# One tap column of a shifted sum: an identity matmul on TensorE against an add on VectorE at PSUM eviction

## The chip, the cores and the metric

The kernel runs on one core of a Trainium2 chip. The metric is the device time of one execution in microseconds (us). The kernel before was timed three times: 4166.49, 4167.12 and 4171.71 us, median 4167.12 us. A fourth execution was profiled.

## What is computed

The input x has shape (4, 128, 128, 128): 4 images, 128 channels, 128 rows of 128 pixels, float32. Two "metaformer" layers follow. Only the first convolution matters here, cut from the reference:

```python
offset = conv3x3(ln_c(x), w_off)            # 18 channels: 9 taps x (dy, dx)
py, px = base_y + dy, base_x + dx           # per tap and pixel
sampled = bilinear_gather(ln_c(x), py, px)  # (B, C, 9, H, W)
x = x + einsum("bckhw,ock->bohw", sampled, w_conv)
# then: a routed mixture of experts, a Fourier mixing, a second expert stage
```

The offsets are a 3x3 convolution with 18 outputs. For one output pixel it is a sum over three tap rows ky and three tap columns kx. The term of tap column kx must be moved by kx-1 pixels along the row.

## The kernel before

The program has phases that run one after the other: a setup, phase A (normalisation, offsets, sampling and the first convolution; up to about 2146 us of the span), a test for far offsets, phase BC and phase DE. The change lies in phase A alone.

**Phase A** works on NG = 128 groups G of four image rows, 32 groups for each image. Pixels of a row lie on the 128 partitions. The function order_a (L169) writes one list of stages with slots of time, and each engine's function (tensor, scalar, vector, gpsimd, sync) walks through that one list and issues its own stages in that order. So each engine's instructions stand in a fixed order, and semaphores join the engines. A step s of the list lasts 12 slots, 18 where the chunk of sampled rows has six rows rather than four (at the end of an image), and touches several groups at once:

- turn, stats, scale, norm and conv for group F = s+4. TensorE transposes the rows into PSUM (L312, tile TK), VectorE takes their statistics (L458, L461), ScalarE writes the normalised rows (L379). TensorE multiplies the rows with the offset weights (L321: 162 = 9 taps x 18 columns) into YB[0] and YB[1]. ScalarE takes them out, scaled, into the ring yr (L406).
- zsum, shift, offs, offs_out, reach, place and hats for group Z = s+2. GpSimd adds the three tap rows of yr into zz (L534, L540), which keeps three tap columns of 18 values for each of 4 rows. TensorE multiplies each tap column with a shift matrix and adds the three in PSUM, tile OF (L330, 72 columns = 4 rows x 18). ScalarE copies OF to on (L417) and sends it to memory (L392). VectorE reduces on to a maximum and a minimum (L467, L468), GpSimd places it into the ring oc (L568, L576) and forms the interpolation weights hh (L552, L555). ScalarE takes their absolute value (bend, L422), VectorE clips them (L473).
- prod and turn_s for the chunk of group N = s+1: VectorE (even rows, L481) and GpSimd (odd rows, L521) multiply the weights into sx, VectorE transposes each into tt (L490).
- sample: TensorE multiplies windows of the normalised image with tt into SB (L351), three parts a quad of rows. ScalarE copies SB to the ring sr (L443).
- out, residual and x1_out for group s-2: nine matmuls of 512 columns into OB (L366), then VectorE adds the input (L496).

The shift matrices come from constants(): shift[:, kx, :] has ones where row x+kx-1 meets column x. For kx = 1 that is the unit matrix.

YO is one PSUM bank that holds YB[1] in columns 0 to 323 and OF in columns 324 to 395 (L261 to L263). So shift waits until ScalarE has emptied YB (y_ready), and conv with h = 1 waits until OF has been taken out (on_ready). The stages around the change before:

```python
elif o[0] == "shift":                      # TensorE, L324
    w.wait_ge(z_step, z_count[G]); w.wait_ge(on_ready, G)
    w.wait_ge(y_ready, 4 * min(G + 2, NG))
    for kx in range(3): matmul(OF, shift[:, kx, :], zz[:, G % 2, :, kx, :])
elif o[0] == "offs":                       # ScalarE, L411
    w.wait_ge(shifted, G + 1); w.wait_ge(on_out[G % 2], 16 * (G // 2))
    w.wait_ge(oc_ready, G - 1); w.wait_ge(reached, 2 * (G - 1))
    copy(on[:, G % 2], OF).then_inc(on_ready, 1)
```

zz and on have two buffers each. GpSimd's zsum of group G waits for shifted of group G-2, since it overwrites that group's zz.

Of the kernel before, what the change touches and what calls it, by code (L numbers as in the profile page):

```python
# [10 lines left out]
ALU = mybir.AluOpType  # L11
# [231 lines left out]
def phase_a(nc, ctx, ins, k, xtp, offd, x1d):  # L243
# [6 lines left out]
    zz = S("a_zz", [128, 2, 4, 3, 18])  # L250
    on = S("a_on", [128, 2, 4, 18])
# [17 lines left out]
    def sem(name):  # L269
        sems.append(ctx.enter_context(nc.semaphore("a_" + name)))  # L270
        return sems[-1]
# [2 lines left out]
    turned, convolved, shifted, sampled, conv_out = (  # L274
        sem(n) for n in ("turned", "convolved", "shifted", "sampled", "conv_out"))

    normed, y_ready, on_ready, bent, sr_ready = (sem(n) for n in ("normed", "y_ready", "on_ready", "bent", "sr_ready"))

    filled, bn_done, mv_ready, reached, clipped, weighed_dve, turned_s, x1_ready = (
        sem(n) for n in ("filled", "bn_done", "mv_ready", "reached", "clipped", "weighed_dve", "turned_s", "x1_ready"))  # L280

    rs_step, z_step, oc_ready, hats_ready, weighed_pool = (
        sem(n) for n in ("rs_step", "z_step", "oc_ready", "hats_ready", "weighed_pool"))
# [3 lines left out]
    on_out = [sem(f"on_out{i}") for i in range(2)]  # L287
# [15 lines left out]
    def tensor(e):  # L303
        w = Once(e)
        for o in order:
            if o[0] == "turn":
                G = o[1]
                w.wait_ge(x_in[G % NX], 16 * (G // NX + 1))
                w.wait_ge(mv_ready, G)
                w.wait_ge(normed, 2 * G)  # L310
                for r in range(4):
                    t = e.transpose(TK[:, r, :], xin[:, G % NX, r * 128:(r + 1) * 128], k["ident"][:, :])  # L312
                t.then_inc(turned, 1)
            elif o[0] == "conv":
                _, G, h = o
                w.wait_ge(y_ready, 4 * (G - 1) + 2 * h + 2)
                if h:

                    w.wait_ge(on_ready, min(G - 2, NG - 1) + 1)
                for r in range(2):  # L320
                    t = e.matmul(YB[h][:, r, :], xin[:, G % NX, (2 * h + r) * 128:(2 * h + r + 1) * 128],  # L321
                                 k["wof"][:, :], start=True, stop=True)
                t.then_inc(convolved, 1)
            elif o[0] == "shift":  # L324
                G = o[1]
                w.wait_ge(z_step, z_count[G])
                w.wait_ge(on_ready, G)
                w.wait_ge(y_ready, 4 * min(G + 2, NG))
                for kx in range(3):
                    t = e.matmul(OF[:, :, :], k["shift"][:, kx, :], zz[:, G % 2, :, kx, :], start=(kx == 0),  # L330
                                 stop=(kx == 2))
                t.then_inc(shifted, 1)
            elif o[0] == "sample":


                _, Q, h = o
                m_ = quad(Q)[1]
                for j in range(2):
                    w.wait_ge(win_in[half_of(Q, j) % NWH], win_count[half_of(Q, j)])
                w.wait_ge(filled, 1)  # L340
                w.wait_ge(turned_s, quad(Q)[0] + m_)
                w.wait_ge(sr_ready, 3 * Q + h)
                for i in range(NWIN // 3):
                    for j in range(2):
                        for q in range(4):
                            u = NU_ * (NWIN // 3 * h + i)
                            m = tt[32 * q:32 * q + 32, Q % NTP, 1152 * j + u:1152 * j + u + 1]

                            m = bass.AP(m.tensor, m.offset, [list(m.ap[0]), [96, 3 * m_], [31, 3], [1, NU_]])
                            d = SB[:, q, 0:432].rearrange("p (k t x) -> p k t x", k=12, t=3)  # L350
                            t = e.matmul(d[:, 0:3 * m_, :, NU_ * i:NU_ * i + NU_],  # L351
                                         win[32 * q:32 * q + 32, half_of(Q, j) % NWH, NWIN // 3 * h + i, :], m,
                                         start=(j == 0), stop=(j == 1))
                t.then_inc(sampled, 1)
            elif o[0] == "out":
                _, G, t_ = o
                w.wait_ge(x1_ready, G)
                w.wait_ge(sr_ready, 3 * quad_of(last_centre(G)) + 3)
                kr, kx = divmod(t_, 3)
                a = (4 * G - 2) % NSR  # L360
                ob = OB[:, :].rearrange("p (r x) -> p r x", r=4)

                m = 4 if a + 4 <= NSR else 2 + kr
                for y, r, m in [(a, 0, m)] + ([(a + m - NSR, m, 4 - m)] if m < 4 else []):
                    rows = sr[:, y * 1152:(y + m) * 1152].rearrange("p (r t x) -> p r t x", r=m, t=9)
                    t = e.matmul(ob[:, r:r + m, :], k["wcv"][:, 3 * (2 - kr) + kx, :], rows[:, :, t_, :],  # L366
                                 start=(t_ == 0 and r == 0), stop=(t_ == 8))
                if t_ == 8:
                    t.then_inc(conv_out, 1)

    def scalar(e):
        w = Once(e)
        for o in order:
# [20 lines left out]
            elif o[0] == "y_out":  # L394
                _, G, h = o
                b, q = divmod(G, GI)
                for r in (2 * h, 2 * h + 1):
                    y = 4 * q + r
                    k0, k1 = max(0, 1 - y), min(3, H + 1 - y)
                    w.wait_ge(convolved, 2 * G + r // 2 + 1)  # L400
                    if G >= 3:
                        w.wait_ge(z_step, z_count[G - 3 if r < 3 else G - 2])
                    for first, slot, m in runs(b * H + y - 1 + k0, k1 - k0, NYR):
                        kr = first - (b * H + y - 1)
                        d = slot * 162 + kr * 54
                        a = e.activation(yr[:, d:d + 216 * m].rearrange("p (k f) -> p k f", f=216)[:, :, 0:54],  # L406
                                         YB[r // 2][:, r % 2, 54 * kr:54 * (kr + m)].rearrange(
                                             "p (k f) -> p k f", f=54),
                                         ACT.Identity, bias=k["zero"][:, 0:1], scale=rs[:, G % 2, 4 + r:5 + r])
                    a.then_inc(y_ready, 1)  # L410
            elif o[0] == "offs":  # L411
                G = o[1]
                w.wait_ge(shifted, G + 1)
                w.wait_ge(on_out[G % 2], 16 * (G // 2))
                w.wait_ge(oc_ready, G - 1)
                w.wait_ge(reached, 2 * (G - 1))
                e.copy(on[:, G % 2, :, :], OF[:, :, :]).then_inc(on_ready, 1)  # L417
            elif o[0] == "bend":
                G = o[1]
                v = hh[:, G % 2, 0:len(chunk(G))].rearrange("p c t i -> p (c t i)")  # L420
                w.wait_ge(hats_ready, G + 1)
                e.activation(v, v, ACT.Abs).then_inc(bent, 1)  # L422
            elif o[0] == "sample":
                _, Q, h = o
                n, m_ = quad(Q)
                b, c = centre(n)
                R = b * H + c - 1
                w.wait_ge(sampled, 3 * Q + h + 1)
                w.wait_ge(conv_out, (min(R + m_ + 1, b * H + H - 1) - NSR) // 4 + 1)

                if c < 0:
                    parts = [(0, 1, 2, 1), (1, 1, 1, 2), (2, 2, 0, 3)]
                elif m_ < 4:
                    parts = [(0, 1, 0, 2), (1, 1, 0, 1)]
                else:
                    parts = [(0, 4, 0, 3)]
                for kx in range(3):
                    x = max(0, 12 * h - kx)
                    m = min(31, 12 * h + 11 - kx) + 1 - x
                    for i, ni, kr, nk in parts:  # L440
                        d = sr[:, ((R - 2) % NSR + i + kr) * 1152 + kr * 384 + kx * 128 + x:][:, 0:1]
                        v = SB[:, 0, (9 * i + 3 * kr + kx) * 12 + x + kx - 12 * h:][:, 0:1]
                        a = e.copy(bass.AP(d.tensor, d.offset, [list(d.ap[0]), [1152, ni], [1536, nk], [32, 4], [1, m]]),  # L443
                                   bass.AP(v.tensor, v.offset, [list(v.ap[0]), [108, ni], [36, nk], [512, 4], [1, m]]))
                a.then_inc(sr_ready, 1)

    def vector(e):
# [4 lines left out]
        for o in order:  # L452
            if o[0] == "stats":
# [5 lines left out]
                for i in range(4):  # L459
                    w.wait_ge(bn_done, 4 * G + i + 1)  # L460
                    a = e.bn_aggr(mv[:, G % 2, i, :], st[:, G % 2, i, :])  # L461
                a.then_inc(mv_ready, 1)
            elif o[0] == "reach":
                G = o[1]
                w.wait_ge(on_ready, G + 1)
# [32 lines left out]
    def gpsimd(e):  # L498
        w = Once(e)
        for o in order:  # L500
# [24 lines left out]
            elif o[0] == "zsum":  # L525
# [3 lines left out]
                z = zz[:, G % 2, :, :, :].rearrange("p r k f -> p r (k f)")  # L529
                n = z_count[G]  # L530
                w.wait_ge(y_ready, 4 * G + (5 if q < GI - 1 else 4))
                w.wait_ge(shifted, G - 1)
                if q < GI - 1:
                    e.tensor_tensor(z, v[:, :, 0, :], v[:, :, 1, :], ALU.add).then_inc(z_step, 1)  # L534
                else:
# [1213 lines left out]
```

## Time and profile before

| | before |
|---|---|
| median of 3 runs | 4167.12 us (4166.49 to 4171.71) |
| profiled execution, its own time | 4168.03 us |
| its span | 4166.2 us |
| mean granted TensorE clock | 0.957 of full speed |
| TensorE matmul busy | 3877.1 us (93%) |
| VectorE busy | 2583.8 us (62%) |
| ScalarE busy | 1772.6 us (43%) |
| GpSimd busy | 1585.4 us (38%) |

The times are of whole executions; the span is from the first to the last instruction of the profiled one. Busy time is the time in which an engine had an instruction under way. TensorE's granted clock has two levels here, 1.0 (2.4 GHz) and 0.5 (1.2 GHz). A float32 matmul stands in the trace as two matmul records and two weight loads, so the three matmuls of a shift are six of each.

### The profile page before, as it was taken

The numbers are of one execution on the slowest core, as the hardware profiler recorded it, in microseconds if no ns is written. First come the engines' busy times: TensorE is split into PE (matmuls) and PEld (weight loads), VectorE is DVE, ScalarE is ACT, GpSimd is POOL, SyncE is SP. The second block draws the span as 40 slices with busy tenths as digits, with TensorE's granted clock in tenths as the row PEclk, the third lists the DMA queues.
The fourth block names the chain that finished last, engine by engine and source line by source line (L and its number), as shares of the span: only waits on it lengthen the run. The fifth ranks groups of instructions, "written<-read, shape, count | busy, mean of one in ns | idle before, by whom it ended". The sixth has DMA issues, their size and how long they took to land. (4 is left out here: it accounts for less than half of the span.)

```text
span 4166.2 us, 90514 instructions
## 1 busy us (share of the span) xinstructions
PE 3877.1 (93%) x32471; PEld 2569.3 (62%) x32471; DVE 2583.8 (62%) x8765; ACT 1772.6 (43%) x4557; POOL 1585.4 (38%) x2857
## 2 busy tenths in 40 slices
PE   4999999999999999999978999999999999986458
PEld 4666666666666666666644555666666666654245
DVE  3444434444444444444428888999999999986634
ACT  3555545555555555555511111333333333356124
POOL 3544445454454544544412222332323232344210
PEclk8999999999999999999989999999999999999755
DMA  5544454444554544545416666777777777754869
GB/s 126 93 89 92 88 88 91 90 90 90 92 92 89 91 90 92 92 87 94 76 56 244 244 246 257 258 261 264 257 268 254 268 257 267 252 174 124 335 263 395
DMA packets 602226, 705.73 MB, mean 169 GB/s; under 512 B 61088, under 2 KB 484768, under 8 KB 585392
## 3 DMA queue, kind: packets, MB, share of 16 engines
q1 hardware_dynamic: 496304, 625.97, 52.6%
q10 hardware_dynamic: 104448, 71.85, 5.7%
q8 instruction: 258, 4.23, 0.5%
q14 instruction: 192, 1.57, 0.1%
q0 software_dynamic: 1024, 2.10, 0.1%
HBM read 519.10 MB, written 179.54 MB: 168 GB/s over the span
## 5 line engine op out<-in xcount | busy, mean ns | idle before, releaser
L366 PE MATMUL a_ob<-a_sr,wcv 128*128 128x512 f32 (+3 forms) x2820 | 1084.4, 519 | 0.8 <-DVE a_xo L496 0.8
L443 ACT COPY a_sr<-a_sb 128x576 f32<-128x576 f32 (+7 forms) x1296 | 620.9, 562 | 914.8 <-PE a_sb L351 906.6
L351 PEld LDWEIGHTS a_sb<-a_tt,a_win 32*128 32x128 f32 x19008 | 655.6, 185 | 260.0 <-issue 244.6
L351 PE MATMUL a_sb<-a_tt,a_win 32*128 32x144 f32 x19008 | 748.2, 300 | 14.5 <-ACT a_sr L443 13.1
L521 POOL TENSOR_TENSOR a_sx<-a_hh 128x576 f32<-128x576 f32 x260 | 378.5, 1456 | 927.3 <-DVE a_hh L473 919.2
L366 PEld LDWEIGHTS a_ob<-a_sr,wcv 128*128 128x128 f32 x2820 | 493.2, 192 | 279.6 <-issue 231.2
L473 DVE TENSOR_SCALAR a_hh<-a_hh 128x576 f32<-128x576 f32 (+1 forms) x128 | 59.5, 465 | 944.0 <-ACT a_hh L422 944.0
L1075 DVE TENSOR_TENSOR b_P<-b_P,b_x 128x1024 f32<-128x1024 f32 x512 | 620.0, 1212 | 0.1
L985 PE MATMUL b_z<-b_P,b_ew 128*128 128x512 f32 x1024 | 475.0, 607 | 0.0
L1206 POOL TENSOR_TENSOR b_ss<-b_st 128x12 f32<-128x12 f32 (+2 forms) x167 | 35.2, 211 | 1124.5 <-DVE b_pp L1150 993.5
L988 PE MATMUL b_z<-b_P,b_ew 128*128 128x512 f32 x1024 | 460.3, 592 | 0.0
L490 DVE STREAM_TRANSPOSE a_tt<-a_sx 128x576 f32<-128x576 f32 x520 | 401.8, 773 | 21.2 <-POOL a_sx L521 12.2
L988 PEld LDWEIGHTS b_z<-b_P,b_ew 128*128 128x128 f32 x1024 | 194.6, 190 | 206.1 <-issue 201.4
L1222 POOL TENSOR_TENSOR b_rs<-b_ss,mhalf 128x12 f32<-128x12 f32 (+2 forms) x167 | 312.4, 1871 | 13.2 <-POOL b_ss L1218 0.2
L1048 ACT ACTIVATE c_tn<-c_x,b_rs 128x128 f32<-128x128 f32 x512 | 163.6, 390 | 349.2 <-POOL b_rs L1222 348.2
L985 PEld LDWEIGHTS b_z<-b_P,b_ew 128*128 128x128 f32 x1024 | 184.5, 190 | 200.1 <-issue 184.8
L379 ACT ACTIVATE a_tn<-a_tk,a_rs 128x128 f32<-128x128 f32 x512 | 195.7, 485 | 8.8 <-POOL a_rs L513 8.8
L481 DVE TENSOR_TENSOR a_sx<-a_hh 128x576 f32<-128x576 f32 x260 | 193.9, 746 | 4.3
L1419 PE MATMUL d_b<-ident,e_x 128*128 128x128 f32 x512 | 137.5, 425 | 47.3 <-DMA e_x<-x3d 46.4
L496 DVE TENSOR_TENSOR a_xo<-a_ob,a_xin 128x512 f32<-128x512 f32 x128 | 88.4, 690 | 122.0 <-PE a_ob L366 122.0
L967 PE MATMUL b_rd<-b_iw,b_x 128*128 128x136 f32 x1024 | 153.8, 294 | 5.5 <-DVE b_lr L1100 3.5
L982 PE MATMUL b_z<-b_pT,b_ebm 32*128 32x128 f32 x1024 | 148.5, 284 | 0.0
(181 smaller groups left out, 5406.3 us busy)
## 6 DMA issues: line engine op xcount, KB each, us to landing
b_P<-pd SPq DMA_DIRECT2D x128, 2048.0 KB, 7.4
a_win<-xtp SPq DMA_DIRECT2D x2144, 36.0 KB
a_xin<-in_x SPq DMA_DIRECT2D x128, 256.0 KB, 5.9
xtp<-a_tn ACTq DMA_DIRECT2D x128, 256.0 KB, 2.3
x1d<-a_xo SPq DMA_DIRECT2D x128, 256.0 KB, 5.7
b_x<-x1d SPq DMA_DIRECT2D x128, 256.0 KB, 7.7
x2d<-b_xa SPq DMA_DIRECT2D x128, 256.0 KB, 2.8
d_wb<-in_w SPq DMA_DIRECT2D x16, 2048.0 KB, 18.8
```

Source lines behind the costliest of these rows:

```text
L351: t = e.matmul(d[:, 0:3 * m_, :, NU_ * i:NU_ * i + NU_], win[32 * q:32 * q + 32, half_of(Q, j) % NWH, NWIN // 3 * h + i, :], m, start=(j = ...
L366: t = e.matmul(ob[:, r:r + m, :], k["wcv"][:, 3 * (2 - kr) + kx, :], rows[:, :, t_, :], start=(t_ == 0 and r == 0), stop=(t_ == 8))
L379: a = e.activation(tn[:, G % NTN, r, :], TK[:, r, :], ACT.Identity, bias=rs[:, G % 2, r:r + 1], scale=rs[:, G % 2, 4 + r:5 + r])
L443: a = e.copy(bass.AP(d.tensor, d.offset, [list(d.ap[0]), [1152, ni], [1536, nk], [32, 4], [1, m]]), bass.AP(v.tensor, v.offset, [list(v.ap ...
L481: e.tensor_tensor(sx[:, n % NST, :, 0:NI * NJ].rearrange("p t (j i) -> p t j i", j=NJ), hh[:, G % 2, i, :, None, 0:NI].to_broadcast([128, ...
L490: e.transpose(tt[:, Q % NTP, 0:2304].rearrange("p (j a t x) -> p a t j x", j=2, a=4, t=9)[:, n - quad(Q)[0]], sx[:, n % NST, :, :].rearran ...
L521: e.tensor_tensor(sx[:, n % NST, :, 0:NI * NJ].rearrange("p t (j i) -> p t j i", j=NJ), hh[:, G % 2, i, :, None, 0:NI].to_broadcast([128, ...
L985: e.matmul(ZE[u][:, :, :], ew[:, x, :], P[:, G % NPB, :, x, :], start=False, stop=False)
L988: t = e.matmul(ZE[u][:, :, :], ew[:, x, :], P[:, G % NPB, :, x, :], start=False, stop=(x == 7))
L1048: f = e.activation(tn3[:, u, r, :], x3t[:, G % 3, r, :], ACT.Copy, scale=rs[:, (G + LAG) % 2, 8 + r:9 + r])
L1075: t = e.tensor_tensor(v, v, x1[:, G % NX1, r, None, :].to_broadcast([128, 8, 128]), ALU.mult)
L1222: e.tensor_tensor(rs[:, u, c], ss[:, u, 2, c], k["mhalf"][:, c], ALU.pow).then_inc(scaled, 1)
```

## The change

TensorE multiplies only tap columns 0 and 2 with their shift matrices. The stage offs moves from ScalarE to VectorE, where it becomes one tensor_tensor: OF plus zz[:, G % 2, :, 1, :], written to on. The waits of offs stay the same; on_ready is now VectorE's. GpSimd's zsum waits for on_ready of group G-2 instead of shifted. Nothing else moves.

```diff
             elif o[0] == "shift":
                 G = o[1]
                 w.wait_ge(z_step, z_count[G])
                 w.wait_ge(on_ready, G)
                 w.wait_ge(y_ready, 4 * min(G + 2, NG))
-                for kx in range(3):
+                for kx in (0, 2):
                     t = e.matmul(OF[:, :, :], k["shift"][:, kx, :], zz[:, G % 2, :, kx, :], start=(kx == 0),
                                  stop=(kx == 2))
                 t.then_inc(shifted, 1)
...
     def scalar(e):
-            elif o[0] == "offs":
-                G = o[1]
-                w.wait_ge(shifted, G + 1)
-                w.wait_ge(on_out[G % 2], 16 * (G // 2))
-                w.wait_ge(oc_ready, G - 1)
-                w.wait_ge(reached, 2 * (G - 1))
-                e.copy(on[:, G % 2, :, :], OF[:, :, :]).then_inc(on_ready, 1)
...
     def vector(e):
+            elif o[0] == "offs":
+                G = o[1]
+                w.wait_ge(shifted, G + 1)
+                w.wait_ge(on_out[G % 2], 16 * (G // 2))
+                w.wait_ge(oc_ready, G - 1)
+                w.wait_ge(reached, 2 * (G - 1))
+                e.tensor_tensor(on[:, G % 2, :, :], OF[:, :, :], zz[:, G % 2, :, 1, :], ALU.add).then_inc(on_ready, 1)
...
     def gpsimd(e):   # zsum
                 w.wait_ge(y_ready, 4 * G + (5 if q < GI - 1 else 4))
-                w.wait_ge(shifted, G - 1)
+                w.wait_ge(on_ready, G - 1)
```

VectorE's own order in a regular step, before (a_xo is the residual, a_sx the product, a_tt the transposed product, fm the maxima and minima):

```order
L496 TENSOR_TENSOR a_xo<-a_ob,a_xin 128x512 [waits a_x1_out0,a_conv_out]
L490 STREAM_TRANSPOSE a_tt<-a_sx 128x9x2x32 [waits a_weighed_pool]
L481 TENSOR_TENSOR a_sx<-a_hh 128x576 [waits a_turned_s]
L490 STREAM_TRANSPOSE a_tt<-a_sx 128x9x2x32 [waits a_weighed_dve]
L467 TENSOR_REDUCE fm<-a_on 128x1 [waits a_on_ready]
L468 TENSOR_REDUCE fm<-a_on 128x1
L490 STREAM_TRANSPOSE a_tt<-a_sx 128x9x2x32 [waits a_weighed_pool]
```

And the same place of a regular step with the change:

```order
L498 TENSOR_TENSOR a_xo<-a_ob,a_xin 128x512 [waits a_x1_out0,a_conv_out]
L492 STREAM_TRANSPOSE a_tt<-a_sx 128x9x2x32 [waits a_weighed_pool]
L464 TENSOR_TENSOR a_on<-a_yo,a_zz 128x72 [waits a_oc_ready,a_reached,a_on_out1,a_shifted]
L483 TENSOR_TENSOR a_sx<-a_hh 128x576 [waits a_turned_s]
L492 STREAM_TRANSPOSE a_tt<-a_sx 128x9x2x32 [waits a_weighed_dve]
L469 TENSOR_REDUCE fm<-a_on 128x1 [waits a_on_ready]
L470 TENSOR_REDUCE fm<-a_on 128x1
```

The eviction now stands between the second transpose and the second product, and it carries the wait for TensorE's shift. ScalarE's order before, in the middle of a regular step:

```order
L443 COPY a_sr<-a_sb 128x4x3x4x10
L417 COPY a_on<-a_yo 128x72 [waits a_oc_ready,a_reached,a_on_out1,a_shifted]
L392 DMA offd<-a_on 128x72 [waits a_on_ready]
L443 COPY a_sr<-a_sb 128x4x3x4x12 [waits a_sampled]
L443 COPY a_sr<-a_sb 128x4x3x4x12 x2
```

And with the change:

```order
L438 COPY a_sr<-a_sb 128x4x3x4x10
L394 DMA offd<-a_on 128x72 [waits a_on_ready]
L438 COPY a_sr<-a_sb 128x4x3x4x12 [waits a_sampled]
L438 COPY a_sr<-a_sb 128x4x3x4x12 x2
```

The copy is gone from ScalarE; the DMA to memory stays in its place and waits for VectorE.

## Rows read from the trace of the kernel before

**Rows 1.** The page: busy time by engine, and granted clock in 40 slices.
```profile
PE 3877.1 (93%) x32471; PEld 2569.3 (62%) x32471; DVE 2583.8 (62%) x8765; ACT 1772.6 (43%) x4557; POOL 1585.4 (38%) x2857
...
PEclk8999999999999999999989999999999999999755
```

**Rows 2.** Stretches of phase A: busy time by engine, clock, DMA share, GB/s.
```profile
1000.00:1500.00 500.00, 497.75 (x5805) 340.44 (x5807) 216.32 (x558) 267.91 (x644) 240.03 (x359) 1.00 0.50 91
...
566.00:582.00 16.00, 13.75 (x209) 11.49 (x208) 5.58 (x16) 5.20 (x32) 4.43 (x9) 0.71 0.56 78
...
1090.00:1106.00 16.00, 13.76 (x241) 9.80 (x243) 6.43 (x17) 5.38 (x32) 6.28 (x11) 1.00 0.56 85
```

**Rows 3.** TensorE's timeline: start, us, instruction; one regular step and two image ends.
```profile
554.12 0.89 PE L330 MATMUL a_yo<-a_zz,shift 128*128 128x72 f32 x6
...
570.33 1.57 PE L351 MATMUL a_sb<-a_tt,a_win 32*128 32x72 f32 x48 [0.92 <-ACT a_sr L443]
...
599.01 0.89 PE L330 MATMUL a_yo<-a_zz,shift 128*128 128x72 f32 x6
...
1004.52 2.74 PE L366 MATMUL a_ob<-a_sr,wcv 128*128 128x512 f32 x6
1007.19 1.88 PE L351 MATMUL a_sb<-a_tt,a_win 32*128 32x144 f32 x48
...
1014.58 0.89 PE L330 MATMUL a_yo<-a_zz,shift 128*128 128x72 f32 x6
1015.30 2.80 PE L366 MATMUL a_ob<-a_sr,wcv 128*128 128x256 f32 x12
1018.04 1.89 PE L351 MATMUL a_sb<-a_tt,a_win 32*128 32x144 f32 x48
...
1025.01 0.82 PE L321 MATMUL a_yo<-wof,a_xin 128*128 128x162 f32 x4
...
1028.77 1.89 PE L351 MATMUL a_sb<-a_tt,a_win 32*128 32x144 f32 x48
1030.59 0.89 PE L330 MATMUL a_yo<-a_zz,shift 128*128 128x72 f32 x6
...
1078.54 0.89 PE L330 MATMUL a_yo<-a_zz,shift 128*128 128x72 f32 x6
...
1117.60 0.66 PE L330 MATMUL a_yo<-a_zz,shift 128*128 128x72 f32 x4
```

**Rows 4.** TensorE's weight loads in the same regular step.
```profile
1014.58 0.74 PEld L330 LDWEIGHTS a_yo<-a_zz,shift 128*128 128x128 f32 x6 [0.16 <-issue]
1015.24 2.46 PEld L366 LDWEIGHTS a_ob<-a_sr,wcv 128*128 128x128 f32 x12
```

**Rows 5.** All instructions of L330, and what TensorE waited for until 2200 us.
```profile
L330 PE MATMUL a_yo<-a_zz,shift x768: 272/275/489, 47.2 to 2082.9; 128*128 128x72 f32 x192
...
PE a_sb L351 <- ACT a_sr L443: 13.1, 15, 1.6
...
PE a_yo L330 <- POOL a_zz L540: 9.0, 5, 4.3
```

**Rows 6.** ScalarE's timeline in the regular step.
```profile
1014.72 1.62 ACT L443 COPY a_sr<-a_sb 128x576 f32<-128x576 f32 x3 [3.19 <-PE a_sb L351]
1016.20 0.26 ACT L417 COPY a_on<-a_yo 128x72 f32<-128x72 f32 x1
1016.49 0.36 ACTq L392 DMA_DIRECT2D offd<-a_on  x1
1020.00 1.76 ACT L443 COPY a_sr<-a_sb 128x576 f32<-128x576 f32 x3 [3.54 <-PE a_sb L351]
...
1024.59 0.69 ACT L422 ACTIVATE a_hh<-a_hh 128x576 f32<-128x576 f32 x1
```

**Rows 7.** VectorE's timeline in the regular step, then GpSimd's last weights.
```profile
1012.87 0.69 DVE L496 TENSOR_TENSOR a_xo<-a_ob,a_xin 128x512 f32<-128x512 f32 x1 [0.55 <-PE a_ob L366]
1013.48 0.77 DVE L490 STREAM_TRANSPOSE a_tt<-a_sx 128x576 f32<-128x576 f32 x1
1014.17 0.75 DVE L481 TENSOR_TENSOR a_sx<-a_hh 128x576 f32<-128x576 f32 x1
...
1016.49 0.23 DVE L467 TENSOR_REDUCE fm<-a_on 128x1 f32<-128x72 f32 x1 [0.75 <-ACT a_on L417]
...
1016.77 0.77 DVE L490 STREAM_TRANSPOSE a_tt<-a_sx 128x576 f32<-128x576 f32 x1
1025.30 0.46 DVE L473 TENSOR_SCALAR a_hh<-a_hh 128x576 f32<-128x576 f32 x1 [7.76 <-ACT a_hh L422]
...
1017.50 0.70 POOL L555 TENSOR_TENSOR a_hh<-a_oc,cy 128x288 f32<-128x288 f32 x1
```

**Rows 8.** The nearest VectorE add of PSUM and SBUF with few elements (setup, L61).
```profile
L61 DVE SCALAR_TENSOR_TENSOR wof<-s_t,wraw x1: 327/327/327, 3.6 to 3.6; 128x162 f32<-128x162 f32 x1
```

More of the change, by code:

```diff
@@ L275, in phase_a @@
         sem(n) for n in ("turned", "convolved", "shifted", "sampled", "conv_out"))
-    normed, y_ready, on_ready, bent, sr_ready = (sem(n) for n in ("normed", "y_ready", "on_ready", "bent", "sr_ready"))
-    filled, bn_done, mv_ready, reached, clipped, weighed_dve, turned_s, x1_ready = (
-        sem(n) for n in ("filled", "bn_done", "mv_ready", "reached", "clipped", "weighed_dve", "turned_s", "x1_ready"))
+    normed, y_ready, bent, sr_ready = (sem(n) for n in ("normed", "y_ready", "bent", "sr_ready"))
+    filled, bn_done, mv_ready, on_ready, reached, clipped, weighed_dve, turned_s, x1_ready = (
+        sem(n) for n in ("filled", "bn_done", "mv_ready", "on_ready", "reached", "clipped", "weighed_dve", "turned_s", "x1_ready"))
     rs_step, z_step, oc_ready, hats_ready, weighed_pool = (
```

## Prediction

> **What bounds the kernel now.** I read the page first. TensorE is busy 93% of the span, the other engines 62% or less [rows 1], but that is a mean over phases, and the change lies in phase A. So I cut phase A into stretches. From 1000 to 1500 us TensorE is busy 497.75 of 500 us at the full clock, while VectorE has 216, ScalarE 268 and GpSimd 240 us of work [rows 2]. The timeline shows how regular it is: the shift of one step starts at 1014.58 us and the next at 1030.59 us, 16.01 us a step, with matmuls back to back between [rows 3]. What TensorE waits for up to 2200 us is short: 13.1 us for ScalarE's copies of the samples, at the start and at the ends of images, and 9.0 us for GpSimd's sum in five early steps [rows 5]. So in phase A almost every nanosecond taken from TensorE's row of work is a nanosecond off the time, and work given to VectorE costs nothing as long as nobody on TensorE's side waits for it.
>
> **What the removed matmul is worth.** There are 768 matmul records of L330 [rows 5], six a step, so 128 steps and three matmuls of two records in each. One matmul in three goes: 256 records and 256 weight loads. The 275 ns that a record lasts [rows 5] is no price, since records overlap. The price is the spacing. Two views give it. The first weight load of the shift starts at 1014.58 and the first of the next group at 1015.24: 0.66 us for six loads, 0.11 us each [rows 4]. The first matmul record starts at 1014.58 and the next group's at 1015.30: 0.72 us for six, which includes the step into the group [rows 3]. Taking two records from the middle leaves the step into the group in place, so I take the loads' spacing: 0.66 / 3 = 0.22 us a step. By the other view it is 0.72 / 3 = 0.24 us. The lower bound is a price by columns alone: three 512-column matmuls (six records) take 1007.19 - 1004.52 = 2.67 us, 0.89 us each [rows 3], and 72 / 512 of that is 0.125 us.
>
> The page "TensorE: Matmul & The Clock Gate" of the Trainium skill has both rules side by side. In "Back-to-back issue gap" a warm matmul costs its columns over 2.4 GHz plus 2.5 ns, in "LDWEIGHTS" a load costs its weight columns over 1.2 GHz. With two passes a record, as the 512-column rows imply, the first rule makes a record 62.5 ns and the removal 16 us; the second makes a load 107 ns and the removal 27 us. The spacing of 0.11 us in this trace sides with the second.
>
> Not all 128 steps count. In the first four, before 90 us, TensorE waits for GpSimd's sum, and a shorter matmul only lengthens a wait somewhere. I take them at nothing. 124 x 0.22 = **27.3 us less**. With 0.24 us and all 128 steps it is 30.7 us, the upper bound; with 0.125 us and 128 steps 16.0 us, the lower.
>
> **What is added to VectorE.** One add a step of 72 elements, PSUM plus SBUF. The trace has none of this size. The nearest rows are L61 with 162 elements, 327 ns [rows 8], and the residual with 512 elements, 0.69 us [rows 7]. The line through both is (690 - 327) / 350 = 1.04 ns an element, which gives 327 - 90 x 1.04 = 0.23 us for 72. Nothing to 0.33 us are the bounds. The wait is the larger thing. VectorE's order is fixed, and the add stands between a transpose that ends near 1014.2 us and the product of L481 that started at 1014.17 us [rows 7]. The shift's last record ended at 1015.47 us [rows 3] and will end some 0.22 us earlier. So VectorE stands still for about 1.0 us, adds until about 1015.5 us, and product, transpose, maxima and last transpose slip by about 1.2 us. The last transpose, now 1016.77 to 1017.54 us, ends near 1018.8 us. Who waits for it on TensorE is the first sample part of the next quad, at 1028.77 us [rows 3]: 10 us to spare. VectorE's next work, the clipping, waits for ScalarE until 1025.30 us anyway, after 7.76 us of idleness [rows 7]. I cost this at nothing; its cover is that idle stretch. GpSimd's product for the odd row uses the same two sx buffers and waits for the transposes; it has the same 10 us.
>
> **What leaves ScalarE.** The copy of 0.26 us at 1016.20 us goes [rows 6]. It was followed by 3.54 us of waiting for TensorE's next sample, so it was hidden: nothing. on_ready comes at about 1015.5 us instead of 1016.46 us. Those behind it (the DMA of the offsets, GpSimd's placing and weights, which ended at 1018.20 us, the bend at 1024.59 us [rows 6, 7]) have their data earlier or at the same time. TensorE's own wait for on_ready stands at the second conv, 1025.01 us [rows 3], 9 us later. GpSimd's changed wait asks for a group two steps back, which has long been done.
>
> **At the ends of images** ScalarE's copies hold TensorE up for up to 0.92 us at a time [rows 3]. The stall is between a sample and its copy, whose distance does not change; the time gained earlier is carried through it. VectorE will stand there up to 7 us behind the shift, and the work behind the add has over 10 us to its sample.
>
> **The sum** against the profiled execution: 4168.03 - 27.3 = 4140.7 us. Its time is 0.9 us above the median of the three runs, 4167.12 us, which gives 4139.8. I say **4140 us**. A difference of 0.2%, 8.3 us, is about what a measurement of this kernel can tell from none.
>
> One term is chance. At the first image end the granted clock was down (mean 0.71), at the second it was not (1.00), with the same idle times of TensorE [rows 2]. From shift to shift over two steps that was 599.01 - 554.12 = 44.89 us against 1117.60 - 1078.54 = 39.06 us [rows 3]: 5.8 us for one drop. The change moves every later image end against whatever sets the clock, so one drop more or less is possible: plus or minus 5.8 us. The three runs lie 5.2 us apart, about one such drop.
>
> **The rivals.**
> 1. *The columns are the price.* If the loads could hide, the removed matmul is worth 0.125 us and the time is 4168.0 - 16.0 = 4152 us. For it: the 512-column rows follow their columns. Against: the loads of this very group are spaced evenly at 0.11 us, and the two remaining matmuls have the same form. Chance 5%.
> 2. *Another wait takes its place.* TensorE finishes its step sooner and then waits for a ScalarE copy, a window's DMA or the residual, and the step stays at 16.0 us: 4168 us. For it: such waits appear as soon as samples follow each other closely (0.92 us at an image end [rows 3]). Against: in a regular step the copies end at 1016.34 us and the next sample starts at 1018.04 us [rows 3, 6], 1.7 us to spare against 0.22; the residual ends at 1013.56 us, and its reader starts at 1015.30 us. Chance 3%.
> 3. *VectorE's new wait reaches TensorE.* Each step VectorE stands 1.0 us and works 0.23 us more. If product and transpose were the last thing that TensorE's next quad waits for, that would be exposed: 124 x 1.23 - 27.3 = 125 us, 4293 us, slower. It decides once those instructions run more than the 10 us late that now lie between last transpose and sample. A lock between VectorE and GpSimd would push that way; GpSimd's product lies beside VectorE's. The page "SBUF — State Buffer" of the Trainium skill, "Who interferes with whom", says that a VectorE instruction with two SBUF inputs and a GpSimd one that reads SBUF exclude each other, and that one with a single SBUF input, as the new add, does not; no row here shows the add. Against the rival: one more product's length is under 2 us, far from 10. Chance 2%.
>
> **How the numbers follow.** 90% for the forecast, 5, 3 and 2% for the rivals. Its own range goes from all 128 steps at 0.24 us with one clock drop less (4168.0 - 30.7 - 5.8 = 4131.5) to 27.3 us less with one drop more (4146.5). The rivals are within the 2 in 10 that may be left out, so the range is 4131.5 to 4147. Faster by over 0.2%: the forecast and rival 1, 95%. Within 0.2%: rival 2, 3%. Slower: 2%.
>
> **What would show it.** L332 with 512 records spaced as before; steps of 15.79 us, shift to shift, instead of 16.01; TensorE still busy for over 99% of a regular stretch; the add at about 0.23 us, with an idle time of about 1 us before it that ends with TensorE; ScalarE's copy gone and its waits for samples as long as before. It would be wrong if steps shorten by 0.13 us (rival 1), if TensorE's waits for ScalarE or DMA grow to some 27 us (rival 2), or if its first sample of a quad waits for VectorE's transposes (rival 3).

## The result and the profile after

| | before | changed |
|---|---|---|
| median of 4 runs each | 4169.41 us (4166.49 to 4172.17) | 4146.88 us (4145.19 to 4148.28) |
| ratio, 95% interval | | 0.9948 [0.9934, 0.9963] |
| profiled execution | 4168.03 us | 4145.51 us |
| its span | 4166.2 us | 4143.7 us |
| mean granted TensorE clock | 0.957 | 0.951 |

The change is faster by 22.5 us; the forecast was 27.3 us and a time of 4140 us. The measured median stands 7 us above that, at the very top of the range. Of these 7 us, 4.8 are a smaller gain. The rest is the base: the forecast started from 4167.12 us, and a fourth run of the kernel before moved its median to 4169.41 us. The regular steps of phase A did what was forecast. What was sized wrongly lies at the ends of the images.

The page of the changed kernel, busy time and clock (answers to [rows 1]):

```profile
PE 3865.7 (93%) x32215; PEld 2550.6 (62%) x32215; DVE 2631.6 (64%) x8893; ACT 1758.8 (42%) x4429; POOL 1597.5 (39%) x2857
...
PEclk8999999999999999999979999999999999999755
```

TensorE has 256 matmul records less, VectorE 128 instructions more and ScalarE 128 less. TensorE's timeline in two regular steps (start, us, instruction; answers to [rows 3]):

```profile
997.39 0.67 PE L332 MATMUL a_yo<-a_zz,shift 128*128 128x72 f32 x4
997.90 2.80 PE L368 MATMUL a_ob<-a_sr,wcv 128*128 128x256 f32 x12
...
1013.18 0.67 PE L332 MATMUL a_yo<-a_zz,shift 128*128 128x72 f32 x4
...
1028.93 0.67 PE L332 MATMUL a_yo<-a_zz,shift 128*128 128x72 f32 x4
```

From shift to shift it is 15.79 and 15.75 us, where it was 16.01 and 15.97 us: 0.22 us a step, the spacing of two weight loads. From the shift to the next group's first record it is 0.51 us now and was 0.72 us [rows 3]. The add on VectorE, all 128 of them, and what VectorE did around it in the regular step (answers to [rows 7]):

```profile
L464 DVE TENSOR_TENSOR a_on<-a_yo,a_zz x128: 193/233/235, 45.1 to 2058.2; 128x72 f32<-128x72 f32 x128
```
```profile
996.30 0.77 DVE L492 STREAM_TRANSPOSE a_tt<-a_sx 128x576 f32<-128x576 f32 x1
998.10 0.23 DVE L464 TENSOR_TENSOR a_on<-a_yo,a_zz 128x72 f32<-128x72 f32 x1 [1.03 <-PE a_yo L332]
998.25 0.93 DVE L483 TENSOR_TENSOR a_sx<-a_hh 128x576 f32<-128x576 f32 x1
999.21 0.78 DVE L492 STREAM_TRANSPOSE a_tt<-a_sx 128x576 f32<-128x576 f32 x1
...
1000.15 0.77 DVE L492 STREAM_TRANSPOSE a_tt<-a_sx 128x576 f32<-128x576 f32 x1
```

The wait of 1.03 us and the add of 0.23 us are the forecast numbers. The last transpose ends at 1000.9 us; TensorE's first sample of the next quad starts at 1011.37 us, still 10 us later. What TensorE waited for from 90 to 2100 us is one line:

```profile
PE a_sb L353 <- ACT a_sr L438: 6.6, 7, 1.0
```

So in this profile no wait took the removed matmul's place, on VectorE or anywhere.

**Where the time went.** I cut both spans at events that both have: the fifth and the last shift, the last residual, the first add of phase BC (L1075, now L1077) and the end. Differences are taken before rounding.

| stretch | before, us | changed, us | difference |
|---|---|---|---|
| start to fifth shift | 90.6 | 88.1 | -2.5 |
| fifth to last shift, 123 steps | 1991.8 | 1969.4 | -22.3 |
| last shift to start of last residual | 67.9 | 66.3 | -1.6 |
| last residual to first add of phase BC | 41.6 | 41.8 | +0.2 |
| first add of phase BC to the end | 1974.3 | 1978.1 | +3.8 |

In the second line 123 steps at 0.22 us should give 27.1 us. What is missing is at the image ends. The three inner ones, two steps each from shift to shift, took 44.89, 39.06 and 39.55 us before, and take 42.35, 42.32 and 42.44 us now: 3.6 us more instead of six times 0.22 us less, so 4.9 us in all. The reason stands in the clock column (ninth from the left: busy time of PE, PEld, DVE, ACT, POOL, then the granted clock). Three stretches of 150 us around the three ends, of before and then of the changed kernel:

```profile
500.00:650.00 150.00, 147.75 (x1715) 103.03 (x1710) 65.00 (x165) 76.07 (x205) 71.15 (x107) 0.95 0.50 89
1000.00:1150.00 150.00, 147.75 (x1797) 102.02 (x1795) 64.16 (x165) 78.91 (x212) 70.64 (x108) 1.00 0.51 91
1530.00:1680.00 150.00, 147.30 (x1795) 102.00 (x1794) 63.81 (x164) 78.10 (x208) 69.87 (x106) 1.00 0.50 92
```
```profile
500.00:650.00 150.00, 148.12 (x1761) 102.64 (x1763) 66.29 (x172) 77.52 (x201) 70.01 (x103) 0.97 0.51 91
1000.00:1150.00 150.00, 148.12 (x1770) 101.91 (x1768) 66.11 (x171) 77.38 (x201) 69.83 (x105) 0.97 0.51 90
1530.00:1680.00 150.00, 148.12 (x1746) 101.73 (x1748) 66.04 (x172) 77.41 (x201) 70.32 (x108) 0.97 0.50 91
```

Before, the clock fell to half at one end of three; now it falls at all three. The single drop of before was also the longer one: it took the mean of its stretch to 0.95, each drop of the changed kernel took it to 0.97.

The tail's 1.6 us go with the clock as well. TensorE from the last shift to the last residual, before, changed, and changed once more (e5 below):

```profile
2082.33:2150.26 67.93, 65.25 (x652) 41.68 (x648) 12.12 (x20) 17.63 (x47) 7.98 (x7) 0.92 0.14 30
2057.52:2123.82 66.30, 63.60 (x650) 40.33 (x646) 12.60 (x20) 17.51 (x46) 8.02 (x7) 0.95 0.14 31
2050.77:2115.75 64.98, 62.28 (x650) 39.07 (x646) 12.60 (x20) 17.50 (x46) 8.03 (x7) 0.97 0.14 31
```

The same work, but for the one matmul, took 67.9 us at a mean clock of 0.92, 66.3 us at 0.95 and 65.0 us at 0.97.

### The profile page after: what moved, and what is told of

It reads as the page before. It is cut to its first block and busy times, and to the rows that moved or that the text cites. A ratio compares the mean times of both kernels' runs of the same rounds, so it can differ in the third digit from the quotient of the medians.

```text
span 4143.7 us, 89876 instructions
## 1 busy us (share of the span) xinstructions
PE 3865.7 (93%) x32215; PEld 2550.6 (62%) x32215; DVE 2631.6 (64%) x8893; ACT 1758.8 (42%) x4429; POOL 1597.5 (39%) x2857
## 5 line engine op out<-in xcount | busy, mean ns | idle before, releaser
L1077 DVE TENSOR_TENSOR b_P<-b_P,b_x 128x1024 f32<-128x1024 f32 x512 | 620.2, 1212 | 0.1
L987 PE MATMUL b_z<-b_P,b_ew 128*128 128x512 f32 x1024 | 486.4, 619 | 0.0
L990 PE MATMUL b_z<-b_P,b_ew 128*128 128x512 f32 x1024 | 460.3, 592 | 0.0
L483 DVE TENSOR_TENSOR a_sx<-a_hh 128x576 f32<-128x576 f32 x260 | 225.2, 866 | 4.3
```

Source lines behind the costliest of these rows:

```text
L483: e.tensor_tensor(sx[:, n % NST, :, 0:NI * NJ].rearrange("p t (j i) -> p t j i", j=NJ), hh[:, G % 2, i, :, None, 0:NI].to_broadcast([128, ...
L987: e.matmul(ZE[u][:, :, :], ew[:, x, :], P[:, G % NPB, :, x, :], start=False, stop=False)
L990: t = e.matmul(ZE[u][:, :, :], ew[:, x, :], P[:, G % NPB, :, x, :], start=False, stop=(x == 7))
L1077: t = e.tensor_tensor(v, v, x1[:, G % NX1, r, None, :].to_broadcast([128, 8, 128]), ALU.mult)
```

## The experiments

Theory: the removed matmul is worth 0.22 us a step, all that was moved is covered, and the rest is half clock at the image ends, which depends on the moment at which an end comes. Rivals: the move to VectorE costs something; the clock falls because of the change itself; the drops have nothing to do with the idle gaps at the ends. The ratios are against the kernel before, run on the same chip beside each batch.

### e1_move: the move alone

```diff
-                for kx in (0, 2):
+                for kx in range(3):
...
-                e.tensor_tensor(on[:, G % 2, :, :], OF[:, :, :], zz[:, G % 2, :, 1, :], ALU.add).then_inc(on_ready, 1)
+                e.tensor_copy(on[:, G % 2, :, :], OF[:, :, :]).then_inc(on_ready, 1)
```
(against the changed kernel)

> The move alone: all three matmuls stay, VectorE copies the sum out of PSUM instead of ScalarE. Theory (TensorE bounds phase A, everything moved is covered): the steps stay at 16.0 us from shift to shift and the time stays at that of the kernel before, within some 6 us for clock drops at image ends. Rival (VectorE's new wait reaches TensorE, and part of the missing gain is there): steps longer than 16.0 us, 4 us or more slower. VectorE should stand about 1 us a step before its copy.

Measured: 4167.56 us median (4165.3 to 4173.65, 11 runs), before 4164.32 us (4160.64 to 4171.4, 15 runs); ratio 1.0010 [1.0001, 1.0019]. VectorE and TensorE in the regular step:

```profile
1014.34 0.23 DVE L464 COPY a_on<-a_yo 128x72 f32<-128x72 f32 x1 [1.25 <-PE a_yo L332]
```
```profile
1013.41 0.89 PE L332 MATMUL a_yo<-a_zz,shift 128*128 128x72 f32 x6
...
1029.42 0.89 PE L332 MATMUL a_yo<-a_zz,shift 128*128 128x72 f32 x6
```

VectorE stands 1.25 us, since the shift is a matmul longer, and the step is 16.01 us, as before. From the fifth shift to the last it is 1991.3 us against 1991.8 us. The move costs TensorE nothing. The three image ends took 44.49, 39.36 and 39.22 us, with the one drop at the first end as in the kernel before. The interval of the whole time lies just above one: the medians are 3.2 us apart, the ratio says 4 us, and that is the second sign that the rival was given. Its first sign, longer steps, is absent, and no stretch of phase A in the profile holds the difference, so I leave it open. The whole change (ratio 0.9948) and e2 (0.9953), which lacks the move, do not show it.

### e2_drop: the matmul alone

```diff
-                for kx in range(3):
+                for kx in (0, 2):
```
(against the kernel before)

> The matmul alone: two matmuls a step, ScalarE copies the sum out as before; the middle tap column is left out of the offsets. Theory (the matmul is worth 0.22 us a step): steps of 15.79 and 15.75 us, 27 us off the steps, and the time 4140 to 4148 us depending on the clock at the image ends. Rival (the columns are the price): 16 us less than before. Rival on the clock (the missing gain comes from VectorE's part): no clock drop at the second and third image end, time near 4137 us.

Measured: 4146.43 us median (4141.43 to 4148.71, 5 runs), ratio 0.9953 [0.9940, 0.9967], the same as the whole change. The steps are 15.79 and 15.75 us, the three image ends take 42.33, 42.29 and 42.35 us, and all three are at half clock for a while:

```profile
500.00:650.00 150.00, 148.12 (x1734) 102.75 (x1734) 62.88 (x160) 80.15 (x213) 69.80 (x105) 0.97 0.49 91
1000.00:1150.00 150.00, 148.12 (x1731) 102.18 (x1729) 62.62 (x162) 79.50 (x213) 69.27 (x103) 0.97 0.51 90
1530.00:1680.00 150.00, 148.12 (x1744) 102.66 (x1737) 63.03 (x158) 79.91 (x212) 70.44 (x108) 0.97 0.48 92
```

The kernel leaves out the middle tap column of the offsets; its other instructions stay. Gain and drops both come without VectorE's part. The rival that VectorE's part caused the drops is out.

### e3_one: one matmul less again

```diff
-                for kx in (0, 2):
-                    t = e.matmul(OF[:, :, :], k["shift"][:, kx, :], zz[:, G % 2, :, kx, :], start=(kx == 0),
-                                 stop=(kx == 2))
+                for kx in (0,):
+                    t = e.matmul(OF[:, :, :], k["shift"][:, kx, :], zz[:, G % 2, :, kx, :], start=(kx == 0),
+                                 stop=True)
```
(against the changed kernel)

> The changed kernel with one matmul instead of two (tap column 2 is left out of the offsets). Theory: another 0.22 us a step, steps of 15.57 and 15.53 us, 27 us less than the changed kernel but for the clock at image ends. Rival (waits of ScalarE's copies or VectorE begin to hold TensorE): steps shorten by less than 0.22 us.

Measured: 4116.39 us median (4110.82 to 4119.34, 4 runs), ratio 0.9888 [0.9873, 0.9903].

```profile
984.25 0.44 PE L332 MATMUL a_yo<-a_zz,shift 128*128 128x72 f32 x2
999.81 0.44 PE L332 MATMUL a_yo<-a_zz,shift 128*128 128x72 f32 x2
1015.33 0.44 PE L332 MATMUL a_yo<-a_zz,shift 128*128 128x72 f32 x2
```

Steps of 15.56 and 15.52 us: the second matmul is worth the same 0.22 us as the first, so nothing else bounds the step within another 0.22 us. Here two image ends kept the full clock (38.59 and 38.17 us) and the third did not (41.91 us). A drop is not a fixed consequence of a shorter step.

### e4_fill: output matmuls between the samples of an image end

```diff
+            last = len(chunk(s)) > 4 if s < NG else False
-            for t, slot in enumerate((1, 2, 3, 5, 6, 7, 9, 10, 11)):
+            for t, slot in enumerate((1, 2, 3, 5, 6, 7, 13, 15, 17) if last else (1, 2, 3, 5, 6, 7, 9, 10, 11)):
                 put(t0 + slot, "out", s - 2, t)
-            put(t0 + 12, "residual", s - 2)
-            put(t0 + 13, "x1_out", s - 2)
+            put(t0 + (18 if last else 12), "residual", s - 2)
+            put(t0 + (19 if last else 13), "x1_out", s - 2)
```
(against the changed kernel)

> The changed kernel with the last three of nine output matmuls of the group put between the closely spaced samples at each image end. Theory (the gain that is missing is half clock at three image ends, 3.7 us each, and the drops come with TensorE's idle gaps there): the gaps of 0.9 us go (some 2 us an image end, four ends), the clock stays at 1.0 at the image ends, and the time falls by about 8 + 11 = 19 us from the changed kernel, to about 4128 us. Rival (clock drops are not tied to these gaps): the gaps go, the drops stay, 8 us.

Measured: 4144.41 us median (4142.99 to 4146.19, 5 runs), ratio 0.9952 [0.9939, 0.9966]: a miss against the 4128 us expected. TensorE's timeline at the first image end:

```profile
561.19 1.58 PE L354 MATMUL a_sb<-a_tt,a_win 32*128 32x72 f32 x48 [0.85 <-ACT a_sr L439]
...
563.76 1.57 PE L354 MATMUL a_sb<-a_tt,a_win 32*128 32x72 f32 x48
565.26 1.12 PE L369 MATMUL a_ob<-a_sr,wcv 128*128 128x512 f32 x2
...
571.15 1.88 PE L354 MATMUL a_sb<-a_tt,a_win 32*128 32x144 f32 x48 [1.77 <-DMA a_win<-xtp]
```

The first wait for ScalarE stayed, at 0.85 us. The later ones went, as meant, and a wait of 1.77 us for the next windows' DMA took their place. The first two ends kept the full clock (39.40 and 39.00 us), the third had a short drop (41.43 us). And the last shift to the last residual took 71.9 us where the changed kernel has 66.3 us. TensorE in that stretch:

```profile
2054.34:2126.20 71.86, 68.66 (x650) 42.46 (x646) 12.60 (x20) 17.49 (x46) 8.01 (x7) 0.88 0.13 28
```

The mean clock there was 0.88 instead of 0.95. The three tails above get about 0.6 us longer for each hundredth of clock lost, so an estimate for 0.88 is some 70 us: most of the longer tail goes with the clock and 1 to 2 us are left for the moved matmuls. Whether the order of the matmuls brought the lower clock was not tested. So the expectation failed in two parts: the stalls were not TensorE's and ScalarE's alone, and at the last end the filling did not pay in this profile.

### e5_again: the changed kernel once more

> The changed kernel once more, beside the next three on one chip. Theory (whether an image end falls into half clock depends on the moment at which it comes): the profile shows either three drops at the image ends or none, since the ends fell alike in the first profile, and the single times lie in two groups, some 11 us apart. Rival (the shorter step itself makes every end drop): three drops again, 42.3 us for each end's two steps, and times within 3 us.

Measured: 4141.49 us median (4137.42 to 4148.32, 5 runs), before 4169.09 us (4163.15 to 4171.1, 9 runs), ratio 0.9943 [0.9929, 0.9956]. The profiled execution took 4137.42 us:

```profile
500.00:650.00 150.00, 147.58 (x1814) 101.59 (x1814) 68.57 (x176) 79.00 (x204) 73.18 (x108) 1.00 0.51 93
1000.00:1150.00 150.00, 147.43 (x1787) 101.10 (x1786) 68.58 (x178) 78.85 (x204) 73.01 (x113) 1.00 0.51 91
1530.00:1680.00 150.00, 147.40 (x1794) 101.30 (x1787) 67.59 (x174) 79.17 (x204) 72.31 (x107) 1.00 0.50 92
```

The same program, and no drop at any of the three ends: 38.83, 38.93 and 39.01 us. From the fifth shift to the last it took 1959.1 us, 10.3 us less than in the first profile. TensorE's timeline at the first image end, in this execution and then in the first profile of the same program:

```profile
564.84 1.57 PE L353 MATMUL a_sb<-a_tt,a_win 32*128 32x72 f32 x48 [0.92 <-ACT a_sr L438]
567.37 1.57 PE L353 MATMUL a_sb<-a_tt,a_win 32*128 32x72 f32 x48 [0.37 <-ACT a_sr L438]
570.08 1.89 PE L353 MATMUL a_sb<-a_tt,a_win 32*128 32x144 f32 x48 [1.13 <-DMA a_win<-xtp]
571.89 0.67 PE L332 MATMUL a_yo<-a_zz,shift 128*128 128x72 f32 x4
```
```profile
561.25 1.75 PE L353 MATMUL a_sb<-a_tt,a_win 32*128 32x72 f32 x48 [0.92 <-ACT a_sr L438]
562.93 1.11 PE L312 MATMUL a_tk<-ident,a_xin 128*128 128x128 f32 x4
563.98 2.85 PE L353 MATMUL a_sb<-a_tt,a_win 32*128 32x72 f32 x48
567.78 3.27 PE L353 MATMUL a_sb<-a_tt,a_win 32*128 32x144 f32 x48 [0.95 <-ACT a_sr L438]
```

The gap of 0.92 us ahead of it is the same in both. At the full clock the third sample takes 1.57 us and then TensorE waits 1.13 us for the windows' DMA; at half clock it takes 2.85 us and no DMA is waited for. So a drop costs less than the matmuls' own lengthening, and the DMA is what e4 ran into. The comparison settles one question: the changed step does not by itself make the clock fall. How often it falls, and whether the change makes that more likely, five profiles do not tell. It also shows a small cost that the first profile does not: at the full clock TensorE waited for the windows' DMA at all three ends, 3.7 us in all, against one such wait of 1.4 us before:

```profile
PE a_sb L353 <- DMA a_win<-xtp: 3.7, 3, 1.3
```

The expected two groups 11 us apart are not seen in the five times, which spread over 4137 to 4148 us; the phases behind phase A vary by some microseconds as well.

### e6_delay1 and e7_delay2: the image ends moved by a fraction of a step

```diff
-                for r in range(4):
+                for r in list(range(4)) * (3 if G == 10 else 1):
                     t = e.transpose(TK[:, r, :], xin[:, G % NX, r * 128:(r + 1) * 128], k["ident"][:, :])
```
(e6; in e7 five times instead of three)

> The changed kernel with the four transposes of group 10 done three times over, 0.87 us of TensorE once, long before the first image end. It shifts all image ends by 0.87 us and changes nothing else. Theory (the moment decides): an end that dropped may stay at full clock; then its two steps take 38.6 us instead of 42.3, and three ends give 11 us. Rival (the work at the ends decides): 42.3 us at each end whatever the delay.

> The same with the transposes done five times over, 1.73 us. Theory (the moment decides): at least one of the two delays shows image ends of 38.6 us with no drop. Rival: 42.3 us at each end in both.

Measured: e6 4145.5 us median (4138.85 to 4156.12), ratio 0.9943 [0.9929, 0.9956]; e7 4147.86 us (4139.07 to 4150.36), ratio 0.9952 [0.9939, 0.9966]; 5 runs each. The delays are in the traces: the step of group 10 took 16.67 and 17.54 us. In e6's profile the three ends took 42.34, 42.31 and 42.40 us, in e7's 38.66, 38.85 and 38.66 us. The clock of the first end, e6 and then e7:

```profile
500.00:650.00 150.00, 148.12 (x1773) 102.92 (x1772) 65.29 (x167) 77.33 (x200) 70.00 (x105) 0.97 0.52 91
```
```profile
500.00:650.00 150.00, 147.75 (x1807) 101.64 (x1810) 68.65 (x176) 79.13 (x204) 73.32 (x109) 1.00 0.49 93
```

Both outcomes again, all three ends alike in each. This does not show that the delay chose between them, since e5 showed that executions of one program fall either way. As a test of the delay the pair is inconclusive.

### e8_best: filled ends for three images only

```diff
-            last = len(chunk(s)) > 4 if s < NG else False
+            last = s < NG - 1 and len(chunk(s)) > 4
```
(against e4_fill)

> The filled image ends, but only for the first three images; the last keeps its order, since filling it made the tail of phase A 5.6 us longer. Theory: two steps at an image end take 39.0 to 39.4 us (41.4 where a short drop comes), the tail 73.9 us again, and the time is 5 to 6 us under the kernel filled at all four ends, 4139 us. Rival (the tail's length came from its clock and not from the order): no gain over 4144 us.

Measured: 4139.74 us median (4132.9 to 4144.44, 5 runs), ratio 0.9929 [0.9915, 0.9943]. The ends took 39.37, 41.58 and 39.78 us. The last shift to the last residual is 67.7 us at a mean clock of 0.92. The kernel before has 67.9 us at the same clock, so this tail is what its clock gives, and the rival, that the tail's length came from its clock, is not excluded. (The expectation counts the tail to the first matmul of the test for far offsets, 7.6 us later: 75.3 us against the 73.9 us expected.) The medians of e8 and e4 stand 4.7 us apart, but the two were run on different chips; against the kernel before beside each they gain 29.4 and 19.9 us, 9.4 us apart, where 5 to 6 us were expected. Against the changed kernel on the same chip e8 is 1.8 us faster, and the intervals overlap. Filling does not shorten an end at the full clock: filled ends took 39.0 to 39.8 us (e4, e8), unfilled ones 38.7 to 39.0 us (e5, e7). Where the clock fell, it was 41.4 and 41.6 us against 42.3 to 42.4 us. So both short drops are at filled ends, which fits a tie between the gaps and the drops without showing it, since unfilled ends kept the full clock too. The kernel of e8 has the lowest median of the complete versions measured here, though not by more than the measurement can tell. The remaining short drop and the wait for the windows are what is left at the ends.

## Why the prediction was right or wrong

- **What bounds phase A**: right. e3 shows that a further matmul is worth as much as the first, so TensorE bounds the step with at least 0.22 us of room to the next limit. The image ends have less room at the full clock, where e5 shows the windows' DMA.
- **The price of the removed matmul**: right. 0.22 us a step, taken from the spacing of the weight loads; measured 16.01 to 15.79 us and 15.97 to 15.75 us. The price by columns (rival 1, 0.125 us) is out. The page "TensorE: Matmul & The Clock Gate" of the Trainium skill, "LDWEIGHTS", has a load at its columns over 1.2 GHz; for 128 columns that is 107 ns, and 27 us for the 256 removed loads, an estimate by that rule. The trace agrees: 0.11 us a load and 0.22 us a step.
- **What is added to VectorE**: right, 0.23 us and a wait of 1.03 us, hidden as e1 shows.
- **Rival 2 and rival 3**: neither, as forecast. In the first profile TensorE waited 6.6 us for ScalarE in all of phase A from 90 us on (5.8 us before), and never for VectorE. Rival 2 is there in small where the clock stays full: 3.7 us of waiting for the windows' DMA in e5, 1.4 us before.
- **The step that failed** is the one on chance, "so one drop more or less is possible: plus or minus 5.8 us", and with it the choice to forecast as many drops as before. Against the profiled execution the sum said 4140.7 us and 4145.5 us came. The table shows that it is this term: 4.9 us in the second line, while the other four lines cancel to 0.1 us. That they cancel is luck. There were two drops more, 3.7 and 3.3 us, and the one that both have was 2.1 us shorter now. I had seen that one image end with the same gaps can drop and another not, and then treated the ends as single throws of which one changes. In the changed kernel they did not behave so: in all five profiles with two matmuls in this step and unfilled ends (the changed kernel twice, e2, e6, e7) the three ends agree, three times all down and twice none. With three matmuls it was the first end alone, both times (before, e1). Why they fall alike stays open. The ends of the changed kernel come at equal distances, 515.2 us twice, but those of e3 do too (504.7 and 504.4 us), and they fell unlike. By the two profiles of one program, all against none is 10.3 us. So from the fifth shift to the last, against this profile of before with its one drop, the change is worth 1991.8 - 1959.1 = 32.7 us when no end of the changed kernel drops, and 22.3 us when all three do; my 27.3 us lay between the two cases and was neither. Without the 5.8 us of before's drop the 32.7 us are 26.9 us: at equal clock the price of the matmul holds.
- The size of one drop, 44.89 - 39.06 = 5.8 us, came from one end of before. In the changed kernel a drop costs 3.4 to 3.5 us (10.3 / 3), with the clock at half for a shorter time. The bound named one drop more and two more came; because each was smaller, the time still lay near the top of the range.
- **A term that was not in the sum**: phases BC and DE, which the change does not touch, took 1974.3 us in the profile before and 1978.1 us after. I counted the profile before as typical, and it was the shortest of ten; executions of the changed kernel had 1978.4 us (e5) and, with the delay, 1984.2 us (e6). What moves these phases was not tried. In the first profile a start that was 2.5 us shorter and a tail 1.6 us shorter hid it. The start took 88.1 to 92.2 us over the ten profiles and was not shorter in e5 (91.7 us), so its 2.5 us are no gain of the change.

Against the two measurements of the changed kernel, 4146.88 and 4141.49 us, the forecast of 4140 us was low by 7 and by 1.5 us. As differences to the kernel before beside them they are 22.5 and 27.6 us, against 27.3 us forecast; by their intervals the two do not contradict each other.

## What to carry to other kernels

When one engine is busy for over 99% of a stretch, price an instruction on it by the spacing of its neighbours in the timeline, never by its duration: here 0.11 us a record against 275 ns. For the float32 matmuls of 72 columns here that spacing is their weight load, so folding the identity product into the eviction (the copy out of PSUM) pays, even though VectorE gets a wait of 1 us a step: VectorE has the room. And when a periodic program shows the half clock at one of several equal places, look at more than one execution before pricing the drop: equal places can fall together.

## What the runs showed of the hardware

**GpSimd beside VectorE.** GpSimd's copy of the offsets, which the change left as it was, tripled. Before and changed (minimum, median, maximum ns):

```profile
L568 POOL COPY a_oc<-a_on x112: 241/245/837, 49.3 to 2084.3; 128x72 f32<-128x72 f32 x112
```
```profile
L570 POOL COPY a_oc<-a_on x112: 242/775/782, 46.1 to 2058.5; 128x72 f32<-128x72 f32 x112
```

The copy now starts just as VectorE's product of two SBUF tensors runs, and ends when that has ended (GpSimd's timeline; VectorE's product, shown above, ended at 999.18 us):

```profile
997.38 1.18 POOL L523 TENSOR_TENSOR a_sx<-a_hh 128x576 f32<-128x576 f32 x1
998.50 0.78 POOL L570 COPY a_oc<-a_on 128x72 f32<-128x72 f32 x1
```

VectorE's product in turn took 0.93 us instead of 0.75 us; it had started at 998.25 us, while GpSimd's own product ran until 998.56 us. A step later the overlap is longer and so is VectorE's product, 1.15 us (GpSimd, then VectorE):

```profile
1013.40 1.18 POOL L523 TENSOR_TENSOR a_sx<-a_hh 128x576 f32<-128x576 f32 x1
1014.03 1.15 DVE L483 TENSOR_TENSOR a_sx<-a_hh 128x576 f32<-128x576 f32 x1
```

Both times VectorE's product ends 0.6 us after GpSimd's has ended. Over this trace 115 products of VectorE start 0.3 us or more inside one of GpSimd's, and each ends 0.61 or 0.62 us after it; in the trace of before none starts inside one. The page "SBUF — State Buffer" of the Trainium skill, "Who interferes with whom", says that such a pair excludes each other and that the second to issue waits for the first. The trace agrees in both directions. It is hidden in this kernel, but a change that moved VectorE's product by about 1 us made another engine's copy 0.53 us longer. In e1, where VectorE only copies, the copy of GpSimd has a median of 706 ns, so it is the moved product and not the add that it meets.

**The clock.** Equal work, with the same idle gap of 0.92 us ahead of it, was granted the full clock or the half one, depending on the execution, and within each profiled execution of the changed kernel all three image ends fell alike. Where the granted clock fell, two steps of the changed kernel cost 3.4 to 3.5 us more. What decides the moment was not isolated.
